# A four-layer graph network on one core: the maximum over partitions through TensorE and VectorE, with new instruction orders

## What is computed

```
L0: qkv = layernorm(h)*gamma1+beta1, 8 heads of 32: softmax(mask(qkv qkv^T/sqrt(32))) qkv; h + that; then + gelu(layernorm W1 + b1) W2 + b2
L1: hw = h W, 4 heads of 64; e_ij = leaky_relu(src_i + dst_j); e -= max_j e; softmax over neighbours; att hw
L2: as L1 with other weights, logits = leaky(src_i + dst_j), softmax over neighbours
L3: q,k,v projections, 4 heads of 64, masked softmax(q k^T/8) v, relu(. Wo + bo)
```

## Time and profile before

| | us |
|---|---|
| median of 3 runs | 4387.51 |
| lowest, highest run | 4381.95, 4387.93 |
| profiled execution | 4386.9 |
| its span, first to last instruction | 4385.0 |

### The profile page before, as it was taken

One profiled execution on the slowest core, in us unless ns is written; L12 is line 12 of the kernel. 1 busy time (PEld: TensorE's weight loads), 2 busy tenths in 40 slices (PEclk: granted clock), 3 DMA queues, 4 the chain that ended last, 5 costly groups with the idle time before them and its releaser, 6 DMA issues.

```text
span 4385.0 us, 59504 instructions
## 1 busy us (share of the span) xinstructions
PE 4098.6 (93%) x22822; PEld 1952.0 (45%) x22884; DVE 3228.5 (74%) x6985; ACT 2161.6 (49%) x3361; POOL 334.5 (8%) x469
## 2 busy tenths in 40 slices
PE   4799999999999999999999999999999999999997
...
GB/s 87 29 44 54 54 20 54 34 54 54 54 20 54 34 54 54 54 20 49 39 54 54 49 25 49 39 54 54 46 28 49 39 54 54 38 36 48 26 30 29
DMA packets 212314, 193.92 MB, mean 44 GB/s; under 512 B 144448, under 2 KB 179008, under 8 KB 203584
## 3 DMA queue, kind: packets, MB, share of 16 engines
...
## 4 chain that ended last, share of the span: by engine, by line
PE 60%; DVE 23%; ACT 9%; issue 4%; DMA 2%; SPq 1%; POOL 0%; POOLq 0%; ACTq 0%; DVEq 0%
PE M L435 10%; DVE PG L1017 7%; PE O L474 6%; PE M L422 6%; PE M L446 6%; PE M L488 5%; PE S L521 5%; DVE x L934 4%; DVE PP L903 4%; PE S L355 3%; PE O L537 3%; PE O L478 3%; ACT PP L622 3%; PE M L579 3%; PE M L413 2%
## 5 line engine op out<-in xcount | busy, mean ns | idle before, releaser
L622 ACT ACTIVATE PP<-S,reach 128x1024 f32<-128x1024 f32 x512 | 542.4, 1110 | 375.1 <-PE S L355 249.0
L1017 DVE SCALAR_TENSOR_TENSOR PG<-g,tcg,mT 128x512 f32<-128x512 f32 x1024 | 692.4, 740 | 12.8 <-DMA g<-t_rows 10.8
L903 DVE TENSOR_TENSOR PP<-PP,mT 128x1024 f32<-128x1024 f32 x512 | 598.6, 1215 | 75.4 <-ACT PP L622 75.4
L474 PE MATMUL O<-PG,V 128*32 128x512 f32 x4096 | 565.1, 646 | 15.3 <-DVE PG L1017 14.6
L647 ACT ACTIVATE z<-x,nb,rs 128x256 f32<-128x256 f32 x384 | 206.6, 596 | 556.6 <-DVE nb L893 556.4
L422 PE MATMUL M<-hT,W 128*128 128x512 f32 x1024 | 460.6, 603 | 2.8 <-ACT hT L657 2.0
L435 PE MATMUL M<-W,H 128*128 128x256 f32 x2048 | 463.0, 380 | 0.0
L435 PEld LDWEIGHTS M<-W,H 128*128 128x128 f32 x2048 | 379.7, 190 | 62.6 <-issue 0.3
L1046 DVE TENSOR_TENSOR PP<-PP,m 128x1024 f32<-128x1024 f32 x256 | 301.5, 1219 | 87.1 <-ACT PP L736 87.1
L1128 POOL TENSOR_SCALAR ve<-mv 128x4 f32<-128x4 f32 x192 | 80.9, 421 | 3456.5 <-DVE mv L861 3109.0
L355 PE MATMUL S<-hT 32*128 32x512 f32 x2048 | 295.0, 645 | 28.7 <-ACT PP L622 27.8
...
## 6 DMA issues: line engine op xcount, KB each, us to landing
g<-t_rows SPq DMA_DIRECT2D x64, 1024.0 KB, 5.7
adj<-adj_in SPq DMA_DIRECT2D x32, 1024.0 KB, 6.0
...
z<-t_rows SPq DMA_DIRECT2D x64, 256.0 KB, 4.0
...
mT<-z SPq DMA_TRANSPOSE x128, 4.4
m<-V SPq DMA_TRANSPOSE x128, 5.4
```

Of the source, the lines that this page charges most:

```text
L474: e.matmul(k.O[0][r:r + 32, :], s.V[:, jt, 64 * hh + 32 * v:64 * hh + 32 * v + 32], p[:, u, :], start=(jt == 0), stop=(jt == NT - 1))
L622: e.activation(p[:, 2 * pair:2 * pair + 2, :], k.S[:, 2 * pair:2 * pair + 2, :], ACT.Exp, bias=k.reach[:, 7:8], scale=SC0).then_inc(k.e0.s ...
L903: e.tensor_tensor(p[:, 2 * pair:2 * pair + 2, :], p[:, 2 * pair:2 * pair + 2, :], s.mT[:, jt:jt + 1, :].to_broadcast([128, 2, N]), ALU.mul ...
L1017: e.scalar_tensor_tensor(out=p[:, u, :], in0=s.T[hh], scalar=s.tcg[:, 1, hh, jt:jt + 1], in1=s.mT[:, jt, :], op0=ALU.max, op1=ALU.mult).th ...
```

## The change

1. GpSimd's `gmax` goes, and with it `amx` and the signal `parg`. In its place come four steps in layers 1 and 2: `gmt` (TensorE) transposes the 128 x 4 maxima into bank M1, `gm4` (VectorE) takes the maximum of each of the 4 rows, `gmd` (VectorE) multiplies a 4 x 4 identity by it, and `gmb` (TensorE) multiplies a 4 x 128 block of ones by that diagonal, so that every partition of M1 holds the four maxima. `gprep` on VectorE reads them there.
2. The semaphores of `trow` and `tbc` are one per buffer for both layers (`nth`).
3. The orders of all five engines are new. A turn's list now starts at another place in the cycle; the batches are renamed to fit. Apart from that the steps stand close to where they stood, with differences that the excerpt shows.

```diff
+    def nth(self, b, i):
+        return self.sems[b % self.n], 16 * (self.per * (b // self.n) + i + 1)
...
+            s.m4 = sb(f"m4{k}", [4, 1])
+            s.dg = sb(f"dg{k}", [4, 4])
...
+    def gmt(self, b, L):
+        e, k, s = self.e, self.k, self.k.of(b)
+        self.wait_ge(k.consts, NCONST)
+        self.wait_ge(*k.gmx[L].at(b, 0))
+        self.take("M1", k.gm4[L].at(b, 0))
+        e.transpose(k.M[1][0:4, 0:128], s.mx[:, 0:4], k.ident[:, :]).then_inc(k.gmt[L].sem, 1)
...
+    def gmb(self, b, L):
+        e, k, s = self.e, self.k, self.k.of(b)
+        self.wait_ge(*k.gm4[L].at(b, 0))
+        self.take("M1", k.gex[L].at(b, 0))
+        e.matmul(k.M[1][:, 0:4], k.unit[0:4, 0, 0:1].to_broadcast([4, 128]), s.dg[:, :], start=True,
+                 stop=True).then_inc(k.gmb[L].sem, 1)
...
+    def gm4(self, b, L):
+        e, k, s = self.e, self.k, self.k.of(b)
+        self.wait_ge(*k.gmt[L].at(b, 0))
+        self.mark(e.tensor_reduce(s.m4[:, :], k.M[1][0:4, 0:128], AX.X, ALU.max), "top", L, b, 0)
...
+    def gmd(self, b, L):
+        e, k, s = self.e, self.k, self.k.of(b)
+        self.marked("top", L, b, 0)
+        e.tensor_scalar(s.dg[:, :], k.ident[0:4, 0:4], s.m4[:, 0:1], None, ALU.mult).then_inc(k.gm4[L].sem, 1)
...
     def gprep(self, b, L):
-        self.wait_ge(*k.parg[L].at(b, 0))
-        top = s.amx[:, 0:4, None].to_broadcast([128, 4, NT])
+        self.wait_ge(*k.gmb[L].at(b, 0))
+        top = k.M[1][:, 0:4, None].to_broadcast([128, 4, NT])
...
-    def gmax(self, b, L):
-        self.wait_ge(*k.gmx[L].at(b, 0))
-        e.partition_all_reduce(s.amx[:, 0:4], s.mx[:, 0:4], 128, bass.bass_isa.ReduceOp.max).then_inc(k.parg[L].sem, 1)
```

```diff
 def sync_program(do):
...
-        do.trow(b3, 2)
-        do.tbc(b3, 2)
-        do.masks_t(b1, 0)
-        do.rrow(b4)
+        do.masks_t(b1, 1)
         do.rbc(b4)
         do.trow(b2, 1)
+        do.loada(b0)
         do.tbc(b2, 1)
         do.store(b4)
-        do.masks_t(b1, 1)
-        do.loada(b0)
         do.load(b0)
+        do.masks_t(b0, 0)
+        do.trow(b2, 2)
+        do.tbc(b2, 2)
+        do.rrow(b3)
```

More of the change, by code:

```diff
@@ L96 @@
     spc=(1, 1, 3), goc=(2, 1, 3), god=(1, 1, 3), qka=4, vva=2, e3=8, oc3=2, od3=1, rdc=1,
-    qt=2, sc0=16, pv0=8, dn0=4, b2r=(4, 0, 3), tt=(2, 0, 4), w1=8, w2=4, pj=(4, 1, 3), srt=(1, 1, 3), gpv=(4, 1, 3), qk=4,
+    qt=2, sc0=16, pv0=8, dn0=4, b2r=(4, 0, 3), tt=(2, 0, 4), w1=8, w2=4, pj=(4, 1, 3), srt=(1, 1, 3), gmt=(1, 1, 3), gmb=(1, 1, 3), gpv=(4, 1, 3), qk=4,
     vp=2, sqm=4, sc3=8, pv3=4, dn3=2, den3=1, rd3=1, wo=2,
-    rs=(1, 0, 6), parg=(1, 1, 3),
+    rs=(1, 0, 6),
 )
@@ L209, in __init__ @@
         (self.mk, self.diag, self.nb, self.zb, self.m0, self.qa, self.qa3, self.add, self.nrm, self.w2a, self.xx,
[L210 to L215, removed]
+         self.pjs, self.gmx, self.gm4, self.gex, self.gv, self.gm, self.mx3, self.sh3, self.m3, self.r3, self.o3,
+         self.woa, self.stat, self.z0, self.v0, self.sqa, self.qtc, self.e0, self.oc0, self.od0, self.y0, self.zr,
+         self.hv, self.gelu, self.pjc, self.gtc, self.spc, self.goc, self.god, self.qka, self.vva, self.e3,
+         self.oc3, self.od3, self.rdc, self.qt, self.sc0, self.pv0, self.dn0, self.b2r, self.tt, self.w1, self.w2,
+         self.pj, self.srt, self.gmt, self.gmb, self.gpv, self.qk, self.vp, self.sqm, self.sc3, self.pv3,
+         self.dn3, self.den3, self.rd3, self.wo, self.rs) = [signal(name) for name in SIGNALS]
     def of(self, b):
@@ L293, in gmax, with gmt, gm4, gmd @@
     def gmax(self, b, L): pass
+    def gmt(self, b, L): pass
+    def gm4(self, b, L): pass
+    def gmd(self, b, L): pass
+    def gmb(self, b, L): pass
     def gprep(self, b, L): pass
@@ L1306, in tensor_program @@
         do.wo(b4, 0)
+        do.gmt(b2, 1)
+        do.gpv(b3, 2, 2)
+        do.gmb(b2, 1)
+        do.gpv(b3, 2, 3)
+        do.grow(b2, 1)
         do.wo(b4, 1)
-        do.grow(b2, 1)
-        do.gpv(b3, 2, 2)
-        do.gpv(b3, 2, 3)
         do.b2r(b3, 2, 0)
@@ new lines, in scalar_program @@
+        do.tt(b3, 3, 0)
+        do.tt(b3, 3, 1)
+        do.sc0(b1, 3)
+        do.qk(b3, 0)
+        do.qk(b3, 1)
+        do.sq3(b3, 0)
+        do.sc0(b1, 4)
+        do.sc0(b1, 5)
+        do.out0(b1, 0)
+        do.qk(b3, 2)
+        do.qk(b3, 3)
+        do.lnz(b2, 2, 0)
+        do.sq3(b3, 1)
+        do.sc0(b1, 6)
+        do.sc0(b1, 7)
+        do.vp(b3, 0)
+        do.lnz(b2, 2, 1)
+        do.lnz(b2, 2, 2)
+        do.vp(b3, 1)
+        do.sc3(b3, 0)
+        do.out0(b1, 1)
+        do.lnz(b2, 2, 3)
```

407 lines of the change are left out of this document (195 added, 212 removed).

## The result

| | us |
|---|---|
| before, median of 4 runs (lowest, highest) | 4387.72 (4381.95, 4390.03) |
| after, median of 4 runs (lowest, highest) | 4434.24 (4433.09, 4435.02) |
| ratio, 95% interval | 1.0106 (1.0094 to 1.0118) |
| span of the profiled execution, before and after | 4385.0 and 4432.9 |

The account below looks back on a forecast made before the run. VectorE paces its full stretch of the turn, TensorE most of the rest. From a span of 4385.0, 8 us off the turns and 5 off filling give 4372, 4374 as execution time; range 4330 to 4430, the forecast's own 4358 to 4388.

Parts of the forecast that it names:

- Step 2: VectorE's full stretch, to the end of sq3(b3,0): gvals, a mask and a bst move in, zb out; 44.3 becomes 46.0 us.
- Step 3: gw(b2,1,0) waits for the broadcast issued behind loada: bounds 0 and 3.4 us, 1.0 taken; the full stretch ends at T+61.0.
- step 4: TensorE behind the full stretch: its remaining set takes 10.6 us, 12.1 before; 0.25 us gained a turn, 8 us in all.
- the price of the exchange on TensorE: Transpose and matmul in layers 1 and 2: 0.11 us for each product, 0.45 us a turn, 14 us in the whole.
- step 7: Ends of the pipeline: filling gains 5 us, mostly the wait for mT's transposes at 104.49; draining 0.
- step 1: TensorE from pj(b2,1,0): wo(b4,1) covers ScalarE's copies, b2r(b3,2,0) starts at T+13.2, not 14.48; VectorE's answer 1.1 us earlier.
- Nobody waits for its length alone: The exchange's path is some 0.5 us longer than the old, but runs beside a gpv or tt, so its length costs nothing.
- The slower rival: At gw(b2,1,0), the load ahead of the broadcast costs in full: 4448, typical case 4411; chance 0.3.
- Steps 5 and 6: rb3 and the rows it needs after m's transposes cost 0, 1.4 us to spare; changed queues cost no wait.

Follow-up runs that it names:

- b1: Changed kernel with loada(b0) behind rbc, ahead of trow, and masks(b0,0) on VectorE ahead of wo(b4,1): 4403.58 us, 1.0026 of the kernel before.
- b2: b1 with gvals(b2,1) on VectorE moved behind gprep(b2,1) as well: 4392.07 us, 0.9996 of the kernel before.
- b3: b2 with gvals(b3,2) and resid0(b2) moved ahead of den3(b4) on VectorE: 4389.21 us, 0.9996 of the kernel before.
- a1: Changed kernel with GpSimd's all-reduce back in place of gmt, gm4, gmd and gmb in both layers: 4449.83 us, 1.0156 of the kernel before.
- d1: b3 with GpSimd's all-reduce in place of the exchange (gmt, gm4, gmd, gmb out): 4406.12 us, 1.0038 of the kernel before.
- f1: e1 with the exchange for layer 1 alone and grow behind both gpv; layer 2 keeps the all-reduce: 4451.25 us, 1.0153 of the kernel before.
- a4: Changed kernel with gvals(b2,1) behind gprep(b2,1) and loada(b0) behind tbc and store: 4397.02 us, 1.0031 of the kernel before.
- a2: Changed kernel with loada(b0) moved behind tbc and store in SyncE's queue: 4410.11 us, 1.0062 of the kernel before.
- c2: Kernel before with masks(b1,0) alone moved ahead of sc0(b2,4), into VectorE's full stretch: 4393.14 us, 1.0014 of the kernel before.
- d0: Kernel before with zb(b2) moved behind sq3(b4,0), out of VectorE's full stretch: 4388.44 us, 0.9998 of the kernel before.
- d2: Kernel before with TensorE's wo(b4,1) moved behind gpv(b3,2,3) and grow between the two gpv: 4416.67 us, 1.0057 of the kernel before.
- e1: d2 with the transposes of the mask, masks_t(b1,1), moved ahead of the store in SyncE's queue: 4359.18 us, 0.9943 of the kernel before.

## Why the prediction was wrong

The steps that failed are the end of VectorE's full stretch (steps 2 and 3, T+61.0), the gain behind it (step 4), with the price of the exchange on TensorE in it, and the ends of the pipeline (step 7). In the turn shown:

| | forecast | measured |
|---|---|---|
| `gw(b2,1,0)` starts | T+21.4 | T+21.48 |
| from there to the end of the full stretch | 39.6 | 40.6 |
| TensorE's set behind it (step 4) | 10.6 | 10.73 |
| from there to the next `pj`, against 60.11 before | 59.7 | 60.39 |

- **The full stretch.** It ended at T+62.1 and not at 61.0. 0.4 us is more work (46.36 for 46.0). 0.6 is a wait that the prediction put at nothing: `nb` at 2177.95 waits 0.59 us for GpSimd's `rs`, in each of the 25 turns, where VectorE had no such wait before. GpSimd's `ve` and `rs` took 1.11 and 1.87 us there, not the 0.23 and 1.04 they take elsewhere. In b1, b2 and b3 this wait is gone.
- **The exchange.** Priced at 0.45 us a turn, 0.11 for each product, it took over twice that. In layer 1 `gmt` moved the next product by 0.20 and `gmb` by 0.31, and a1 and d1, without them, have VectorE's answer 0.55 us earlier, where the forecast's price is 0.22. In layer 2 it is 0.11, a wait of 0.19 and 0.31. The product that the price was taken from, `grow` before, moves the next by 0.20 (2108.99 to 2109.19), as step 1 itself has it. The length was put at 0.5 us more than the old path; it is 3.7 more (4.3 against 0.6), since each of its four steps queues behind others.
- **Who waits for that length.** "Nobody waits for its length alone" doesn't hold in the order of before: in f1 `gw(b2,1,0)` waits 2.6 us a turn for the broadcast, and the run is 92 us slower, with the order of after around the exchange. In after `gw(b2,1,0)` stands at T+21.5 and not at T+17.0, behind `gvals` and the statistics, and of this wait 0.54 us is left. The prediction had both numbers (20.4 and 1.0), so the length is not why the forecast was off in the turn. It may be why these orders gain nothing, since `gw(b2,1,0)` had to be moved behind it; that is argued, and no run has the new orders with the all-reduce and an early `grow`.
- **Step 1**: `b2r` at T+13.2, measured T+13.69: the two products and `gpv`, which took 2.72 us with its neighbours and not 2.6. VectorE's answer came 0.55 us earlier, not 1.1. By itself this cost the turn next to nothing, since `gw(b2,1,0)` waited for the broadcast and started at T+21.48, forecast 21.4.
- **Step 2**: both moves stand in it with 1.2 us each; a4 against a2 and b2 against a4 show 13 us for `gvals` and 5 to 15 for the mask, since waits for TensorE and ScalarE take the place of part of the work. The 2.8 us moved in came out of idle time: VectorE's longest wait, ahead of the denominators of layer 3 while TensorE runs `w1`, is 262.4 us in 32 times before and 492.8 after. That the full stretch sets the pace held for what the forecast used it for, work added: c2 shows it. It does not hold for work taken out (d0).
- **Step 3**: the load landed at T+18.1, as forecast, and the broadcast at T+21.4 (2143.15), forecast 21.6. The Trainium skill's rule (DMA: Bandwidth & Descriptors, "HWDGE ordering") that descriptors are consumed in ring order gave this order. The trace agrees: the broadcast landed 3.3 us behind the load, where the bound for that case had 3.5 and a wait of 1.2. The wait was 0.54 in this turn and 34.5 in 32 times, for 1.0 forecast. The slower rival (waits of 2.2 to 3.4 us, 4411 to 4448) named this place, and the time fell between its two; but the wait that came is a quarter of that or less, so it was not that rival's mechanism that decided.
- **Step 4**: the slack of 1.5 us in TensorE's set was there (12.13 us before, 10.73 after). Behind it some 0.4 us were to be gained, and 0.28 were lost. 0.4 of this miss is the exchange in layer 2, 0.61 for the 0.2 of the forecast. The rest is not pinned to a row.
- **Steps 5 and 6**: `rb3` waits for z 12.8 us in 9 times (7.0 in one before), next to nothing, as foreseen, and no wait on the queues showed. That a store ahead of the transposes can cost 50 us, as d2 against e1, isn't in them: the new lists had put the transposes elsewhere.
- **Step 7**: filling was to gain 5 us and lost 1.7; the transposes' wait at 104.49 went, as foreseen, but `pj` comes at 131.45 and not 129.72, and why stays open. Draining was to cost nothing and cost 9.7. Some 5 of this go with the exchange: draining takes 180.5 us in after and 175.4 in a1, 177.7 in b3 and 173.1 in d1. Another place shows: TensorE's first `gpv` of layer 2 in the last batch waits 7.14 us for `gvals` in after and 3.02 for a `gw` before; b3's order brings draining from 181.0 (b2) to 177.7. The rest of it stays open.

The turn was 1.18 us longer in the mean and not 0.25 shorter: 31 x 1.43 = 44 us of the miss. The ends of the pipeline are 16 more. By the one turn shown it would be 31 x 1.78 = 55. The measured 4434 lies 4 us above the range. It isn't settled what else lies between b3 (0.9996) and e1 (0.9943): the exchange and all other differences of order are in it together.
